# Q's first block from exact codes, an earlier copy of the attention's output, and one block of Q's products ahead of O's first unit

## The chip, the cores and the metric

The kernel runs on one core of a Trainium2 chip. The metric is the time of one execution on the device in microseconds (us), the median of several runs. PE is TensorE (PEld its weight loads), DVE is VectorE, ACT is ScalarE, POOL is GpSimd and SP is SyncE, which here only issues DMAs.

## The reference

One decoder layer on x of shape (2, 512, 1024): attention with 32 query and 8 key/value heads of width 128 and weights given as 4-bit codes with one scale for each block of 128 input rows and each output column, a product with a quantised context, and a layer with binarised weights.

```python
def _dequant(codes, scales):
    w = codes.astype(jnp.float32) - 8.0
    return w * jnp.repeat(scales, GS, axis=0)          # GS = 128

q = hidden_states @ _dequant(q_codes, q_scales)         # k and v likewise
...
q = _rope(q); k = _rope(k)
k = jnp.repeat(k, rf, axis=1); v = jnp.repeat(v, rf, axis=1)
scores = jnp.einsum('bhqd,bhkd->bhqk', q, k) * scale + mask[None, None]
attn = jax.nn.softmax(scores, axis=-1)
out = jnp.einsum('bhqk,bhkd->bhqd', attn, v)
return out.transpose(0, 2, 1, 3).reshape(b, s, NH * HD) @ _dequant(o_codes, o_scales)
...
x = x + attn(layernorm(x))
x = x + matmul(fake_quant(layernorm(x)), fake_quant(ctx))
x = x + einsum('bsi,oi->bso', layernorm(x), binarize(weight))
```

## The kernel before

Most of the time goes into 64 **slots**, one for each pair of head and batch: p = 8g + i, with the key/value head g, the head h = i // 2 of its four, and the batch b = i % 2, so that even slots have b = 0. Slots 8 to 39 (g from 1 to 4, a hardware loop) also quantise a piece of the context; they are called context slots here. Slots 0 to 7 and 40 to 63 (g = 5 to 7) prepare the last layer's weights instead; they are called weight slots. Every engine has its own instruction stream, written out by hand in its own `slot` function, and the streams meet in semaphores. There is no scheduler: the order in the text is the order on the engine.

Values are kept as two float16 halves, upper and lower, and a product of two such numbers is three matmuls (`three_products`: upper x upper, upper x lower, lower x upper). A code itself is exact in one half, so a product with it is two matmuls (O's units do that).

In slot p, PE computes: the scores of p in three parts (`scores` 0, 1, 2, into a pair of PSUM banks that alternate), four of O's units of older heads (`o_unit`, 4 matmuls each; the first of them has index 3 of slot p-1), Q's products for slot p+2 (`q_part`: blocks 0 to 7 of the input, 3 matmuls each, 24 in all, summed in PSUM bank `q_ps`), and at the end the product of the probabilities of slot p-1 with V (`weigh`, 12 matmuls, into `pv_ps`). `scores` 2 of a slot waits for ACT's first exponential of the same slot, whose bank it takes.

Between these, for each slot: DVE takes the maxima of the scores (`maxima`), adds O's units to `x_acc` (`o_add`), scales Q's weights (`piece_scale`) and makes their lower half (`piece_lo`). ACT takes the exponentials (`exps`), makes upper halves of the weights (`q_cut`), of Q (`q_hi`), of the probabilities (`prob_split`, parts 0 and 1) and of the attention's output (`ao_part`), and turns O's codes into float16 (`o_cut`). POOL normalises the probabilities (`norm`, four instructions), makes their lower half (`prob_rest`, parts 0 and 1) and that of Q (`q_lo`). In weight slots DVE also runs `wf_lower` and `wf_difference`, POOL `wf_clip` and `wf_add`. `ao_rest` on DVE makes the lower half of the attention's output from `pv_ps`.

The rotary step on Q of slot p+2 runs after its last product: ACT swaps the halves (`q_swap`, two copies of 64 rows), POOL multiplies by the sine (`sine`), DVE by the cosine in place in `q_ps` (`q_cos`), and in the next slot DVE adds the two into `rot` (`q_sum`), ACT and POOL split `rot` into `q_sb` (`q_hi`, `q_lo`). The first product of Q's next slot waits for `q_sum`, which frees `q_ps`.

## Time and profile before

| | us |
|---|---|
| median of 3 runs | 1098.23 (1096.35 to 1099.12) |
| the profiled execution | 1096.75 |
| span of its trace, first to last instruction | 1095.0 |
| PE busy | 1050.8 (96%) |
| DVE busy | 930.0 (85%) |
| POOL busy | 721.3 (66%) |
| ACT busy | 692.5 (63%) |
| PE's granted clock, mean | 0.998 of full speed |
| 32 context slots | 387.9, 12.12 each |
| 22 weight slots, 40 to 61 | 263.9, 12.00 each |

The end of one slot is seen best in `weigh`, of which there is one for each slot. The first slots begin at about 183 us, slot 63 ends at about 946 us; before them lie the layer norm and the products of K and V, behind them the last two layers. A row of a timeline gives start, duration, engine, line and names; in brackets stands how long the engine was idle before it, and which instruction ended that. On ACT, DVE and POOL the recorded duration of an instruction reaches some 0.03 to 0.1 us into the next one, so a step is read from start to start.

### The profile page before, as it was taken

The page shows a single profiled execution, that of the slowest core. Times are in us where ns is not written, and L with a number is a line of the kernel's source. Part 1 is how long each engine was busy: PE and PEld are TensorE (multiplying, and loading weights), DVE is VectorE, ACT ScalarE, POOL GpSimd, SP SyncE. Part 2 cuts the span into 40 slices and gives each one's busy share as a digit, 9 for nine tenths or more (in the row PEclk, how much of TensorE's full clock was granted, in tenths as well). Part 3 has the DMA queues.
Part 4 walks back from the last instruction along what each step waited for, and adds up shares of the span by engine and source line. Part 5 has one row for each costly group of instructions (what it writes and reads, how often), then busy time and mean ns, then how long its engine had stood idle before and what let it go on. Part 6 is the DMA issues. An engine that isn't in the chain of part 4 may idle for free.

```text
span 1095.0 us, 18877 instructions
## 1 busy us (share of the span) xinstructions
PE 1050.8 (96%) x5416; PEld 507.9 (46%) x5416; DVE 930.0 (85%) x1738; ACT 692.5 (63%) x1499; POOL 721.3 (66%) x789
## 2 busy tenths in 40 slices
PE   5999998999999999999999999999999999889998
PEld 3433433455444444444444444445444544444443
DVE  7967998799888888888888889999999998888873
ACT  5536766766777777777777776666666666463320
POOL 4659887877777677767776777788778877332200
PEclk9999999999999999999999999999999999999999
DMA  9664321777776676667666766777867665532443
GB/s 340 205 162 147 97 73 40 166 146 158 154 161 135 156 155 159 137 154 161 151 139 155 161 148 132 153 158 156 149 157 167 143 134 118 108 117 57 99 98 84
DMA packets 309652, 155.74 MB, mean 142 GB/s; under 512 B 257712, under 2 KB 270256, under 8 KB 309584
## 3 DMA queue, kind: packets, MB, share of 16 engines
q1 hardware_dynamic: 301808, 141.56, 56.6%
q10 hardware_dynamic: 7776, 13.37, 4.4%
q8 instruction: 31, 0.51, 0.2%
q14 instruction: 37, 0.30, 0.1%
HBM read 89.07 MB, written 4.19 MB: 85 GB/s over the span
## 4 chain that ended last, share of the span: by engine, by line
PE 73%; DVE 9%; ACT 6%; POOL 5%; issue 3%; DMA 1%; ACTq 1%; SPq 1%; DVEq 0%; POOLq 0%
PE side_ps L721 9%; PE side_ps L893 9%; PE side_ps L723 9%; PE side_ps L722 9%; PE proj_ps L913 8%; PE out_ps L913 8%; PE proj_ps L1064 4%; PE score_ps L876 3%; PE score_ps L877 2%; PE score_ps L878 2%; PE proj_ps L1069 2%; PE score_ps L1035 2%; DVE stats L1755 1%; ACT prob L1240 1%; DVE x_acc L2022 1%
## 5 line engine op out<-in xcount | busy, mean ns | idle before, releaser
L1587 POOL TENSOR_TENSOR w_b<-prob,w_b 128x896 f16<-128x896 f32 (+2 forms) x192 | 189.0, 999 | 29.8 <-ACT w_b L1267 29.5
L721 PE MATMUL side_ps<-hT,w_a 128*128 128x512 f16 x504 | 191.1, 379 | 1.5 <-DVE rot L1942 1.5
L723 PE MATMUL side_ps<-hT,w_a 128*128 128x512 f16 x504 | 191.0, 379 | 0.0
L722 PE MATMUL side_ps<-hT,w_a 128*128 128x512 f16 x504 | 191.0, 379 | 0.0
L1580 POOL TENSOR_SCALAR prob<-prob,row_inv 128x512 f32<-128x512 f32 (+3 forms) x256 | 170.9, 682 | 23.3 <-DVE row_inv L2095 17.9
L2022 DVE SCALAR_TENSOR_TENSOR x_acc<-proj_ps,o_now,x_acc 128x1024 f32<-128x1024 f32 x120 | 153.5, 1279 | 38.3 <-PE proj_ps L913 38.3
L1240 ACT ACTIVATE prob<-score_ps,neg_max 128x512 f32<-128x512 f32 (+3 forms) x256 | 133.0, 522 | 47.3 <-DVE neg_max L1998 39.0
L1594 POOL TENSOR_TENSOR q_sb<-rot,q_sb 128x512 f16<-128x512 f32 x62 | 72.3, 1167 | 137.3 <-ACT q_sb L1230 137.3
L2022 DVE SCALAR_TENSOR_TENSOR x_acc<-out_ps,o_now,x_acc 128x1024 f32<-128x1024 f32 x120 | 152.6, 1272 | 0.0
L913 PE MATMUL out_ps<-work,w_b 128*128 128x512 f16 x496 | 127.3, 379 | 2.0 <-DVE x_acc L2022 2.0
L913 PE MATMUL proj_ps<-work,w_b 128*128 128x512 f16 x496 | 127.3, 379 | 1.9 <-DVE x_acc L2022 1.1
L1998 DVE CUSTOM_DVE_ANT_0 score_ps<-score_ps,mask_b 128x512 f32<-128x512 f32 (+3 forms) x256 | 121.9, 496 | 2.0 <-PE score_ps L878 2.0
L1267 ACT ACTIVATE w_b<-prob 128x896 f16<-128x896 f32 (+2 forms) x192 | 99.5, 552 | 32.7 <-POOL prob L1580 30.5
L893 PE MATMUL side_ps<-work,v_sb 128*128 128x512 f16 (+3 forms) x768 | 114.8, 299 | 0.0
L1575 POOL TENSOR_TENSOR swapped<-swapped,sin_t 128x512 f32<-128x512 f32 x77 | 99.9, 1297 | 0.1
L893 PEld LDWEIGHTS side_ps<-work,v_sb 128*128 128x128 f16 (+1 forms) x768 | 69.7, 98 | 44.8 <-DMA work<-w_b 0.4
L1276 ACT ACTIVATE work<-side_ps 128x512 f16<-128x512 f32 x64 | 38.2, 597 | 72.5 <-PE side_ps L893 72.4
L876 PE MATMUL score_ps<-k_sb,q_sb 128*128 (+4 forms) x256 | 76.9, 300 | 4.7 <-ACT prob L1240 2.2
L721 PEld LDWEIGHTS side_ps<-hT,w_a 128*128 128x128 f16 x504 | 49.2, 98 | 65.7 <-issue 10.8
L723 PEld LDWEIGHTS side_ps<-hT,w_a 128*128 128x128 f16 x504 | 49.3, 98 | 59.5
L913 PEld LDWEIGHTS out_ps<-work,w_b 128*128 128x128 f16 x496 | 48.3, 98 | 61.1 <-DVE x_acc L2022 3.5
L877 PE MATMUL score_ps<-k_sb,q_sb 128*128 (+4 forms) x256 | 76.6, 299 | 0.0
(259 smaller groups left out, 2108.6 us busy)
## 6 DMA issues: line engine op xcount, KB each, us to landing
stage_c<-in_codes_dram SPq DMA_DIRECT2D x72, 256.0 KB, 2.9
stage_o<-in_codes_dram SPq DMA_DIRECT2D x64, 256.0 KB, 3.9
stage_s<-in_scales_dram SPq DMA_DIRECT2D x64, 256.0 KB, 3.8
ctx_raw<-in_ctx_dram ACTq DMA_DIRECT2D x32, 256.0 KB, 3.3
work<-w_b SPq DMA_TRANSPOSE x261, 3.0
x_acc<-in_x_dram SPq DMA_DIRECT2D x8, 512.0 KB, 8.3
k_sb<-in_codes_dram SPq DMA_DIRECT2D x16, 256.0 KB, 7.0
v_sb<-in_scales_dram SPq DMA_DIRECT2D x16, 256.0 KB, 7.2
```

Source lines behind the costliest of these rows:

```text
L721: pe.matmul(o, stat(0), mov(0), start=first, stop=False)
L722: pe.matmul(o, stat(0), mov(1), start=False, stop=False)
L723: return pe.matmul(o, stat(1), mov(0), start=False, stop=last)
L876: pe.matmul(o, q[0], k[0], start=True, stop=False)
L893: mm = pe.matmul(pv_ps[:, kb * P:S], v_sb[:, bass.ds(g, 1), l, b * TB + kb, :].rearrange("p a d -> p (a d)"), probT[:, m, at:kb + (TB - 1) ...
L913: mm = pe.matmul(o[:, b, :], o_codes[:, h % RING, cb * P:(cb + 1) * P], ao[:, h % 2, l, b * S:(b + 1) * S], start=l == 0, stop=l == 1)
L1240: ins = act.activation(prob[:, SCORE_AT[qb]:SCORE_AT[qb] + w], score_ps[:, score_bank(i, u), off:off + w], ACT.Exp, bias=neg_max[:, c:c + ...
L1575: pool.tensor_tensor(y, y, sin_t[:, :], ALU.mult).then_inc(done, 1)
L1580: return pool.tensor_scalar(prob[:, at:at + w], prob[:, at:at + w], row_inv[:, col:col + 1], P_UP, ALU.mult, ALU.mult)
L1587: ins = pool.tensor_tensor(prob16[:, 1, to:to + w], prob[:, at:at + w], prob16[:, 0, to:to + w], ALU.subtract)
L1998: ins = dve.tensor_tensor_reduce(s, s, mask_b[:, S - w:S], -1.0, MAX_FROM, ALU.add, ALU.min, neg_max[:, c:c + 1])
L2022: ins = dve.scalar_tensor_tensor(y, u, s, y, ALU.mult, ALU.add)
```

## The change

1. **Exact codes.** From Q's slot 4 on (`by_parts`), block 0 of Q's weights is kept as codes minus 8 in the upper half alone. PE multiplies it in two matmuls instead of three (`q_exact`), into `pv_ps` instead of `q_ps`. ACT scales the result with the column scales while it copies it to SBUF (`q_base`; the tile is the second half of `stage_o`), DVE adds the sum of blocks 1 to 7 to it (`q_join`). ACT's `q_swap` and the cosine then read SBUF. The cosine moves from DVE (`q_cos`) to POOL (`q_turn`, in the next slot), `q_sum` adds two tiles of SBUF. In every second slot `piece_scale` and `piece_lo` cover 384 columns instead of 512, and ACT's piece is two instructions (128 and 384 columns).
2. **ACT's order.** `ao_part` stands ahead of `q_swap`, which now waits for `q_join`; `o_cut` moves from behind `prob_split` 1 to ahead of `prob_split` 0; `q_hi` moves behind the last exponential.
3. **PE's order.** Block 1 of Q stands ahead of O's unit 0, block 0 and block 2 behind it, all ahead of `scores` 2; before, one block stood there.
4. **DVE's and POOL's order.** `ao_rest` of slot p-2 stands behind the first maxima of slot p instead of at the end of slot p-1; `q_sum` stands behind the last maxima; `piece_lo` behind `o_add` 1. On POOL `sine` and `q_turn` stand at the slot's start, `q_lo` behind the first two norms.
5. O's codes have one buffer instead of two, loaded once `o_cut` has read it. One DMA more (Q's scales, 128 x 256 words) and three small DVE instructions fill a table ahead of the slots.

```diff
+EXACT = P
+EARLY = 2
+Q_LEAD = 3
@@ SyncE @@
+            sp.dma_start(q_scale_rows, q_scales).then_inc(scale_rows_landed, 16)
...
+            def next_o(g, i):
...
+                sp.wait_ge(o_codes_done, p + 1)
+                load_o(o_index(*after), (i + 1) % 2)
@@ TensorE @@
+            def q_exact(g, i):
+
+                h = i // B
+                p = g * SLOTS + i
+                pe.wait_ge(piece_done, g * SLOTS + (2 * h + 2))
+                pe.wait_ge(ao_ready, p - 3)
+                for l in range(2):
+                    mm = pe.matmul(pv_ps, w_a[:, 0, h % RING * KB * P:(h % RING * KB + 1) * P],
+                                   hT[:, l, 0, i % B * S:(i % B + 1) * S], start=l == 0, stop=l == 1)
+                mm.then_inc(q_exact_done, 1)
...
-                        pe.wait_ge(q_summed, p)
+                        pe.wait_ge(q_joined, p - FIRST_PIECES)
...
                     pe.wait_ge(ao_ready, p)
+                if not (known(p) and (p == 0 or p >= N_SLOTS - FIRST_PIECES + 1)):
+                    pe.wait_ge(q_based, p)
...
+                if has_ahead and parts:
+                    q_part(*ahead, range(1, EARLY))
                 if has_o:
                     o_unit(p, i, 0)
-                if has_ahead:
+                if has_ahead and parts:
+                    q_exact(*ahead)
+                elif has_ahead:
                     q_part(*ahead, range(0, 1))
+                if has_ahead and parts:
+                    q_part(*ahead, range(EARLY, 3))
                 scores(p, i, g, 2)
-                if has_ahead:
+                if has_ahead and not parts:
                     q_part(*ahead, range(1, 3))
@@ ScalarE @@
+                if by_parts(p):
+                    act.wait_ge(q_joined, p - FIRST_PIECES + 1)
+                swap(q_swap_of(p), q_sum_in if by_parts(p) else q_bank(p), q_swapped)
+
+            def q_base(g, i):
+
+                p = g * SLOTS + i
+                act.wait_ge(q_exact_done, p - FIRST_PIECES + 1)
+                if not (known(p) and p == FIRST_PIECES):
+                    act.wait_ge(q_cosed, p)
...
+                act.activation(q_sum_in, pv_ps, ACT.Copy, scale=o_now[:, (i // B + 1) % 2, CB:CB + 1])\
+                    .then_inc(q_based, 1)
@@ GpSimd @@
+            def q_turn(p):
+
+                pool.wait_ge(q_joined, p - FIRST_PIECES + 1)
+                pool.wait_ge(q_ready, p)
+                pool.tensor_tensor(rot[:, :], q_sum_in, cos_t[:, :], ALU.mult).then_inc(q_cosed, 1)
@@ VectorE @@
-                dve.tensor_tensor(q_rot(p), q_bank(p), q_swap_of(p), ALU.add).then_inc(q_summed, 1)
+                dve.tensor_tensor(q_rot(p), rot[:, :] if by_parts(p) else q_bank(p), q_swap_of(p), ALU.add)\
+                    .then_inc(q_summed, 1)
+
+            def q_join(p):
+
+                dve.wait_ge(q_done, p + 1)
+                dve.wait_ge(q_based, p - FIRST_PIECES + 1)
+                dve.tensor_tensor(q_sum_in, q_bank(p), q_sum_in, ALU.add).then_inc(q_joined, 1)
```

The order on ACT in a weight slot, from `exps` 2 to the first exponential of the next slot (`stage_s` to `w_a` is the piece, `stage_o` to `w_b` is `o_cut`, `prob` to `w_b` is `prob_split`, `side_ps` to `work` is `ao_part`, into `swapped` goes `q_swap`). Before:

```order
L1240 ACTIVATE prob,row_sum<-score_ps,neg_max 128x256
L1143 ACTIVATE w_a<-stage_s 128x512
L1302 ACTIVATE w_b<-w_b 128x256
L1267 ACTIVATE w_b<-prob 128x896
L1148 ACTIVATE swapped<-side_ps 64x512
L1149 ACTIVATE swapped<-side_ps 64x512
L1276 ACTIVATE work<-side_ps 128x512
L1267 ACTIVATE w_b<-prob 128x128
L1267 ACTIVATE w_b<-prob 128x256
L1253 ACTIVATE w_b<-stage_o 128x512
L1240 ACTIVATE prob,row_sum<-score_ps,neg_max 128x512
```

and with the change:

```order
L1294 ACTIVATE prob,row_sum<-score_ps,neg_max 128x256
L1284 ACTIVATE q_sb<-rot 128x512
L1182 ACTIVATE w_a<-stage_s 128x512
L1356 ACTIVATE w_b<-w_b 128x256
L1307 ACTIVATE w_b<-stage_o 128x512
L1321 ACTIVATE w_b<-prob 128x896
L1330 ACTIVATE work<-side_ps 128x512
L1187 ACTIVATE swapped<-stage_o 64x512
L1188 ACTIVATE swapped<-stage_o 64x512
L1321 ACTIVATE w_b<-prob 128x128
L1321 ACTIVATE w_b<-prob 128x256
L1294 ACTIVATE prob,row_sum<-score_ps,neg_max 128x512
```

The swap now lies behind `ao_part` and ahead of `prob_split` 1, and O's codes are cut before both.

The order on POOL in a weight slot, from `prob_rest` 0 (128x896) of one slot to the norms of the next (`wf_add` and `wf_clip` are `w_b` from `w_b`, 128x256). Before:

```order
L1587 TENSOR_TENSOR w_b<-prob,w_b 128x896
L1575 TENSOR_TENSOR swapped<-swapped,sin_t 128x512
L1587 TENSOR_TENSOR w_b<-prob,w_b 128x128
L1587 TENSOR_TENSOR w_b<-prob,w_b 128x256
L1673 TENSOR_TENSOR w_b<-w_b 128x256
L1648 TENSOR_SCALAR w_b<-w_b 128x256
L1594 TENSOR_TENSOR q_sb<-rot,q_sb 128x512
L1580 TENSOR_SCALAR prob<-prob,row_inv 128x512
L1580 TENSOR_SCALAR prob<-prob,row_inv 128x384
```

and with the change:

```order
L1644 TENSOR_TENSOR w_b<-prob,w_b 128x896
L1644 TENSOR_TENSOR w_b<-prob,w_b 128x128
L1644 TENSOR_TENSOR w_b<-prob,w_b 128x256
L1736 TENSOR_TENSOR w_b<-w_b 128x256
L1632 TENSOR_TENSOR swapped<-swapped,sin_t 128x512
L1652 TENSOR_TENSOR rot<-stage_o,cos_t 128x512
L1711 TENSOR_SCALAR w_b<-w_b 128x256
L1637 TENSOR_SCALAR prob<-prob,row_inv 128x512
L1637 TENSOR_SCALAR prob<-prob,row_inv 128x384
L1657 TENSOR_TENSOR q_sb<-rot,q_sb 128x512
```

The sine has moved behind `prob_rest` 1, the cosine is new behind it, and `q_lo` has moved behind two norms.

The order on DVE in a weight slot, from the last maxima to the last `o_add`. Before:

```order
L1998 ISA score_ps,neg_max<-score_ps,mask_b 128x256
L1998 ISA neg_max 128x1
L2095 RECIPROCAL row_inv<-row_sum 128x3
L1782 SCALAR_TENSOR_TENSOR stage_s<-stage_c,stage_s 128x512
L2099 RECIPROCAL row_inv<-row_sum 128x1
L1966 SCALAR_TENSOR_TENSOR w_b<-w_b 128x256
L1788 SCALAR_TENSOR_TENSOR w_a<-stage_s,w_a 128x512
L2022 SCALAR_TENSOR_TENSOR x_acc<-out_ps,o_now,x_acc 128x1024
L1960 SCALAR_TENSOR_TENSOR w_b<-w_b,wf_mean 128x256
L2022 SCALAR_TENSOR_TENSOR x_acc<-proj_ps,o_now,x_acc 128x1024
```

and with the change:

```order
L2081 ISA score_ps,neg_max<-score_ps,mask_b 128x256
L2081 ISA neg_max 128x1
L2010 TENSOR_TENSOR rot<-rot,swapped 128x512
L2187 RECIPROCAL row_inv<-row_sum 128x3
L1850 SCALAR_TENSOR_TENSOR stage_s<-stage_c,stage_s 128x512
L2191 RECIPROCAL row_inv<-row_sum 128x1
L2049 SCALAR_TENSOR_TENSOR w_b<-w_b 128x256
L2105 SCALAR_TENSOR_TENSOR x_acc<-out_ps,o_now,x_acc 128x1024
L1856 SCALAR_TENSOR_TENSOR w_a<-stage_s,w_a 128x512
L2043 SCALAR_TENSOR_TENSOR w_b<-w_b,wf_mean 128x256
L2017 TENSOR_TENSOR stage_o<-side_ps,stage_o 128x512
L2105 SCALAR_TENSOR_TENSOR x_acc<-proj_ps,o_now,x_acc 128x1024
```

`q_sum` stands ahead of the reciprocals that POOL's norms wait for, and `piece_lo` (L1856) behind an `o_add`.

## Rows read from the trace of the kernel before

**Rows 1.** The page: busy time, share of the span and instructions of each engine.

```profile
PE 1050.8 (96%) x5416; PEld 507.9 (46%) x5416; DVE 930.0 (85%) x1738; ACT 692.5 (63%) x1499; POOL 721.3 (66%) x789
```

**Rows 2.** The chain that ended last, in order of time: start us, us, what.

```profile
220.36 1.63 PE side_ps L893 x12
232.26 1.63 PE side_ps L893 x12
...
268.23 1.63 PE side_ps L893 x12
...
656.12 1.64 PE side_ps L893 x12
...
920.02 1.64 PE side_ps L893 x12
...
1010.88 3.45 PE score_ps L1035 x16
```

**Rows 3.** Timeline of PE in a context slot: start us, us, engine, line, operation.

```profile
318.00 0.38 PE L876 MATMUL score_ps<-k_sb,q_sb 128*128 x1
...
321.94 0.28 PE L876 MATMUL score_ps<-k_sb,q_sb 128*128 x1
```

**Rows 4.** Timeline of ACT in the same context slot.

```profile
318.28 0.60 ACT L1276 ACTIVATE work<-side_ps 128x512 f16<-128x512 f32 x1 [1.18 <-PE side_ps L893]
318.77 0.61 ACT L1267 ACTIVATE w_b<-prob 128x128 f16<-128x128 f32 x2
319.28 0.62 ACT L1253 ACTIVATE w_b<-stage_o 128x512 f16<-128x512 int32 x1
...
321.11 0.69 ACT L1240 ACTIVATE prob<-score_ps,neg_max 128x512 f32<-128x512 f32 x1 [0.69 <-ACT k_sb L1363]
```

**Rows 5.** Timeline of POOL in a weight slot.

```profile
777.73 1.26 POOL L1575 TENSOR_TENSOR swapped<-swapped,sin_t 128x512 f32<-128x512 f32 x1
779.26 1.06 POOL L1587 TENSOR_TENSOR w_b<-prob,w_b 128x128 f16<-128x128 f32 x2 [0.27 <-ACT w_b L1267]
780.28 0.74 POOL L1673 TENSOR_TENSOR w_b<-w_b 128x256 f32<-128x256 f32 x1
780.98 0.41 POOL L1648 TENSOR_SCALAR w_b<-w_b 128x256 f32<-128x256 f32 x1
782.92 1.16 POOL L1594 TENSOR_TENSOR q_sb<-rot,q_sb 128x512 f16<-128x512 f32 x1 [1.54 <-ACT q_sb L1230]
784.32 3.02 POOL L1580 TENSOR_SCALAR prob<-prob,row_inv 128x512 f32<-128x512 f32 x4 [0.23 <-DVE row_inv L2095]
787.60 1.90 POOL L1587 TENSOR_TENSOR w_b<-prob,w_b 128x896 f16<-128x896 f32 x1 [0.26 <-ACT w_b L1267]
```

**Rows 6.** Timeline of DVE in the same weight slot.

```profile
778.71 0.69 DVE L2038 SCALAR_TENSOR_TENSOR work<-side_ps,work 128x512 f16<-128x512 f32 x1 [0.37 <-ACT work L1276]
779.32 0.69 DVE L1998 CUSTOM_DVE_ANT_0 score_ps<-score_ps,mask_b 128x512 f32<-128x512 f32 x1
...
783.98 0.17 DVE L2095 RECIPROCAL row_inv<-row_sum 128x3 f32<-128x3 f32 x1
```

**Rows 7.** Groups on DVE, weight slots 656.12 to 920.02: busy us, mean ns, idle before.

```profile
L1966 DVE SCALAR_TENSOR_TENSOR w_b<-w_b 128x256 f16<-128x256 f32 x21 | 14.7, 702 | 0.0
L1788 DVE SCALAR_TENSOR_TENSOR w_a<-stage_s,w_a 128x512 f16<-128x512 f32 x20 | 13.8, 692 | 0.5 <-ACT w_a L1143 0.5
L1782 DVE SCALAR_TENSOR_TENSOR stage_s<-stage_c,stage_s 128x512 f32<-128x512 int32 x20 | 13.1, 656 | 0.0
```

**Rows 8.** Single lines of DVE with both inputs in SBUF: duration ns min/median/max.

```profile
L1813 DVE TENSOR_TENSOR rot<-rot,swapped x15: 671/693/1752, 78.3 to 174.3; 128x512 f32<-128x512 f32 x15
L1960 DVE SCALAR_TENSOR_TENSOR w_b<-w_b,wf_mean x31: 466/469/1705, 184.1 to 938.8; 128x256 f32<-128x256 f32 x31
```

**Rows 9.** Timeline of DVE: the first maxima of slots 62 and 63.

```profile
922.92 0.69 DVE L1998 CUSTOM_DVE_ANT_0 score_ps<-score_ps,mask_b 128x512 f32<-128x512 f32 x1
...
932.26 0.68 DVE L1998 CUSTOM_DVE_ANT_0 score_ps<-score_ps,mask_b 128x512 f32<-128x512 f32 x1
```

More of the change, by code:

```diff
@@ L462, in build @@
         cc_ready = sem("cc_ready")
-        xs_landed = [sem(f"xs_landed{t}") for t in range(TT)]
         y_turned = sem("y_turned")
@@ L1338, in slot @@
                 exps(p, i, 2)
+                if has_next and by_parts(p + 1):
+                    q_hi(p + 1)
                 if has_piece:
@@ L1344, in slot @@
                     wf_sign(wf_early(p))
+                o_cut(p, i)
                 prob_split(p, 0)
@@ L1348, in slot @@
                     act.activation(ctx_raw[:, :], ctx_raw[:, :], ACT.Copy, bias=ROUND).then_inc(ctx_rounded, 1)
+                if has_prev and not (known(p) and p == N_SLOTS - 1):
+                    ao_part(p - 1, (i - 1) % SLOTS)
                 if has_ahead:
@@ L1356, in slot @@
                     return
-                if has_prev:
-                    ao_part(p - 1, (i - 1) % SLOTS)
                 prob_split(p, 1)
-                o_cut(p, i)
                 if with_ctx:
@@ L1691, in body @@
                     norm(2).then_inc(norm_done, 1)
+                    if not (known(p) and p >= N_SLOTS - 1) and by_parts(p + 1):
+                        q_lo(p + 1)
                     if with_ctx:
@@ L2075, in slot @@
                     j = o_scales(g, i)
-                if i or known(p):
+                first = not (i or known(p))
+                if not first:
+                    maxima(p, i, 0)
+                if first:
+                    dve.wait_ge(q_ready, p + 1)
+                if has_prev and p_ge2:
+                    ao_rest(p - 2, (i - 2) % SLOTS)
+                if first:
                     maxima(p, i, 0)
@@ L2091, in slot @@
                 maxima(p, i, 2)
+                if has_next and by_parts(p + 1):
+                    q_sum(p + 1)
                 if known(p) and p < 3:
@@ L2101, in slot @@
                     wf_lower(wf_late(p))
-                if has_piece:
-                    piece_lo(n, i % 2, q_region(i), Q_UP)
                 if has_o:
                     o_add(p, i, 1)
+                if has_piece:
+                    piece_lo(n, i % 2, q_region(i), Q_UP, (EXACT, 0)[i % B])
                 if known(p) and wf_early(p) is not None:
                     wf_difference(wf_early(p))
+                if has_ahead and by_parts(p + Q_AHEAD):
+                    q_join(p + Q_AHEAD)
                 if has_o:
```

107 lines of the change are left out of this document (65 added, 42 removed).

## Prediction

> **What bounds the kernel now.** Read the page's busy times first: PE is busy for 96% of the span, DVE for 85% [rows 1]. Then read the chain in order of time for the spacing of `weigh`, one in each slot. The closest neighbours are 11.90 us apart (220.36 to 232.26), and this is PE without a pause: 40 matmuls of 512 columns at 0.216 (16 of them take 3.45) are 8.64, `weigh` is 1.63, and the scores have as many columns as `weigh` [rows 2]. So 11.90 is PE's floor. Context slots, 268.23 to 656.12, take 387.89 for 32, or 12.12 each; the 22 weight slots up to 920.02 take 263.90, or 12.00 each [rows 2]. The loop is bound by PE, with 0.22 and 0.10 lost in a slot. Where a context slot loses it the timeline shows: with T for the start of `scores` 0, `scores` 2 begins at T + 3.94 (318.00, 321.94) [rows 3], while the work ahead of it (scores 1.30, two O units 1.73, one block 0.65, all at 0.216 for a full matmul [rows 2]) ends at T + 3.68. It starts 0.83 after the first exponential (T + 3.11) does [rows 4]: PE waits for ACT there.
>
> **The change, part by part.**
>
> *PE.* Two matmuls instead of three in 60 slots (2 to 61) are 60 x 0.216 = 12.9 us where PE is the bound. The floor goes to 11.90 - 0.22 = 11.68. With one more matmul pair and two more blocks, less the old one, `scores` 2 now comes naturally at T + 1.30 + 1.73 + 1.29 + 0.43 = T + 4.75.
>
> *ACT, context slots.* Behind `weigh`, ACT ran `ao_part` (T + 0.28), `prob_split` 1, `o_cut` (0.52 from start to start), the context's last copy, a DMA issue and the exponential [rows 4]. Now the swap's two copies come in, and `o_cut` leaves. For a copy I take `ao_part`'s 0.60 without a gap, so 1.21 for both. The exponential begins at T + 3.11 + 1.21 - 0.52 = T + 3.80, and `scores` 2 may start 0.83 later, at T + 4.63. PE comes at 4.75: no wait, with 0.12 to spare. Other waits of a context slot: POOL runs `prob_rest` 1 at T + 2.7 (0.7 behind the split, which starts at T + 1.99), the sine from T + 3.7, the new cosine until T + 6.3. DVE can be there at T + 5.5 and waits, adds, and its slot still closes by T + 12.3, that is 0.6 into the next slot, before scores are there for it (0.85: 0.65 of matmuls and the tail of the last). `q_lo` ends near T + 10.1, ahead of PE's next slot at 11.68. The context slots go to the floor: 387.89 - 32 x 11.68 = **14.1 us less**. `q_base` (a copy from PSUM, 0.60) and the split piece hide in ACT's idle time, 37% of the span [rows 1]; without it they would push the exponential by up to 0.8.
>
> *Weight slots.* The same walk, from rows of one such slot. POOL: `prob_rest` 1 at T + 2.7, its step 1.02 and `wf_add` 0.70 to T + 4.4, then sine and cosine, 1.27 each less an overlap of 0.03: done at T + 6.9. The cosine has no row in the slots; the sine, the same operation on the same size, is the nearest, and I take its time [rows 5]; a tenth more moves everything below by 0.1. DVE: from the first maxima to the reciprocal is 4.66 (779.32 to 783.98), with a `q_sum` in it (0.61 by its step) that an `ao_rest` of the same step (778.71 to 779.32) replaces [rows 6]. DVE could be at `q_sum` by T + 0.85 + 4.66 = T + 5.5, so it waits until T + 6.95. Behind it stand, by steps (durations less 0.08): `q_sum` 0.61 (0.693), two reciprocals 0.17, `piece_scale` 0.58 and `piece_lo` 0.54 (from 0.656 and 0.692, three quarters in every second slot), `wf_lower` 0.62 (0.702), `wf_difference` 0.40 (median 0.469), `q_join` 0.61 (as long as `ao_rest`, which also reads PSUM), half of an `o_now` copy 0.16, and two `o_add` of 1.19: 6.07 [rows 6 to 8]. The last two, and all O units below, have no row of their own: an `o_add` is what is left of the 4.66 behind three maxima and a `q_sum`, halved. So maxima begin at T + 13.0, 1.35 into the next slot. `ao_rest` is done at 1.35 + 0.60 + 0.69 = 2.64, ahead of O's first unit at 2.81, which waits for it in odd slots. By this the weight slots are at the floor, by 0.17.
>
> What could use up those 0.17 is the meeting of DVE and POOL. An addition with both inputs in SBUF took 0.693 us as median, but up to 1.752, and `wf_difference` 0.469, but up to 1.705 [rows 8]; the first is as fast as `ao_rest` with an input in PSUM (0.69) [rows 6] when nothing is in its way. In the change `q_sum` becomes such an addition and starts as the cosine ends, when POOL goes straight on to `wf_clip` (0.41) [rows 5]: up to 0.33 more. `piece_lo`, now behind an `o_add`, begins at about T + 10.5. POOL gets its reciprocal at T + 8.2, takes two norms of 0.75 (3.02 for four) and is in `q_lo` (1.16) from T + 9.7 to 10.9 [rows 5]: up to 0.4 more. With both, `ao_rest` is done at 2.64 + 0.73 = 3.37 and the unit waits 0.6 in every odd slot, so a pair takes 2 x 11.68 + 0.6 = 24.0, and a slot 12.0. The rows bound this cost between 0 and 1.24 (1.705 less 0.469) for each of these instructions. I take the overlaps as they fall in the walk, because rows 8 show that such instructions do wait: 22 slots at 12.0 are 264.0, **nothing gained or lost**. The four slots 4 to 7 (47.87) are of the same kind: 0. Slots 2 and 3 give 2 x 0.216 = **0.4 less**.
>
> The Trainium skill bears on this (SBUF — State Buffer, section "Who interferes with whom"): a DVE instruction with two SBUF inputs and a GpSimd instruction that reads SBUF take the same read interface, and whichever is second waits until the first is finished. The maxima of rows 8 agree with it, the medians show how rarely it happened. By the rule the weight slots come out at 12.0, without it at 11.68.
>
> *The end.* Slot 62 has no Q products, so it is short: its first maxima and those of slot 63 are 9.34 apart [rows 9]. With the change DVE must wait for the cosine in it until T + 6.95, and then still has `q_sum` 0.94, reciprocals 0.17, `wf_lower` 0.4, `o_add` 1.19, `wf_difference` 0.40 behind POOL's `q_lo` (about 0.9 of waiting), `o_add` 1.19 and the copy: maxima at T + 12.4 against 1.2 in slot 62, so 11.2 apart: 1.9 more. Slot 63 also has two `ao_rest` in place of one, 0.6. PE waits for `q_lo` meanwhile (T + 10.7). **2.5 us more.** Nothing reduces this, since the end of the slots is bound by DVE.
>
> *Costed at nothing.* DVE's three small instructions and the added DMA lie ahead of the slots beside PE's products of K; their bounds are 0 and 3 x 0.4 us. The single buffer of O's codes: loading starts at T + 10.3 and is needed one slot later. The change in SP's order leaves each load several us.
>
> **Sum:** -14.1 + 0 - 0.4 + 2.5 = -12.0 us. Against the profiled execution's 1096.75 this is 1084.8; that execution lies 1.5 under the median 1098.23, so the median becomes **1086.2**.
>
> **The rivals.**
>
> *B, POOL and DVE don't meet.* Then the weight slots reach 11.68: 263.9 - 257.0 = 6.9 less, slots 4 to 7 1.2 less, together -20.1: 1078.1. For it speaks the median of 0.693; against it that the cosine's end releases `q_sum` and `wf_clip` together. 0.15.
>
> *C, a second wait in the context slots.* The spare 0.12 ahead of `scores` 2 is thin. If the swap, the split piece or the context's clip (which moved behind `q_lo`) costs 0.2 more than walked, each of 32 slots gives 0.2 back: -12.0 + 6.4, 1092.6. For it: before, PE waited 0.26 in this very place. 0.19.
>
> *D, slower.* POOL's longest instruction, `prob_rest` 0, reads SBUF and takes 1.90 [rows 5]. In the walk `wf_difference` starts at T + 11.5 and `prob_rest` 0 at T + 12.5. If DVE lags 1.0 more than walked, `wf_difference` or `piece_lo` falls behind it and waits about half, 0.95, in each of 26 weight slots; from then on each lag brings the next. -12.0 + 24.7 = +12.7: 1110.9. For it: an excess of 1.24 does occur [rows 8]. Against it: PE's wait holds both engines back equally, so the phase between DVE and POOL scarcely drifts. 0.12. The Trainium skill's rule in the section named above would make the wait the whole rest of POOL's instruction, up to 1.90.
>
> **How the numbers follow.** The forecast has 0.54. What a measurement of this kernel can tell from no change is about 0.3%, 3.3 us, so "faster" means under 1094.9. Faster: 0.54 + 0.15 + 0.13 of C = 0.82. Same: 0.06 of C. Slower: 0.12. The range takes in B and C with the bounds of the meeting costs and leaves out D and the edges of C: 1077.5 to 1096.
>
> **What would show it.** Context slots: `weigh` 11.68 apart over all 32, no idle on PE ahead of `scores` 2. Weight slots: even slots 11.7, odd ones about 12.3, PE idle ahead of O's first unit with DVE's `ao_rest` as its releaser, DVE's `q_sum` released by POOL's cosine and about 0.3 longer than in context slots. Slot 62 near 11 us instead of 8.5. If context slots show 11.9, C holds; if weight slots show 11.7 throughout, B; if `wf_difference` has a mean over 1 us, D. The forecast is wrong altogether if `q_lo` becomes what `scores` 0 waits for in ordinary slots, since then POOL's chain sets the period.

## The result, and the profile after

The changed kernel takes 1103.95 us (1101.56 to 1108.18) against 1097.78 (1096.35 to 1099.12) for the kernel before: a ratio of 1.006, with a 95% interval of 1.004 to 1.0081. Forecast were 1086.2, with 1077.5 to 1096.0 as the range. So the forecast was wrong in sign: 12 us less was expected, and it became 6 us more. The profiled execution took 1102.88. One execution of the second experiment took 1559.15 us at a mean granted clock of 0.656, where its other three had 0.995 to 0.997; it is left out, and the time given there, 1087.91, is the median of those three, where a later expectation has 1088.6 with it.

First the page, as in [rows 1], with the shares of the chain and a line from its table of queues (packets, MB, share), which was `q14 instruction: 37, 0.30, 0.1%` before:

```profile
PE 1040.0 (94%) x5346; PEld 503.7 (46%) x5356; DVE 957.8 (87%) x1741; ACT 726.5 (66%) x1589; POOL 784.1 (71%) x849
...
q14 instruction: 68, 0.56, 0.2%
...
POOL 50%; issue 17%; DVE 13%; PE 13%; ACT 3%; DMA 1%; SPq 1%; POOLq 0%; DVEq 0%; ACTq 0%
```

PE works 10.8 us less, as intended. DVE is busy 27.8 us longer with three instructions more. That is the first hint: some instruction of DVE has become long.

Where in the program the time goes is read from the starts of `weigh`, as in [rows 2]. PE's timeline of the changed kernel, at the same three borders:

```profile
268.62 1.79 PE L923 MATMUL side_ps<-work,v_sb 128*128 128x512 f16 x12
...
658.06 1.79 PE L923 MATMUL side_ps<-work,v_sb 128*128 128x512 f16 x12
...
922.98 1.79 PE L923 MATMUL side_ps<-work,v_sb 128*128 128x512 f16 x12
```

| from `weigh` to `weigh` | before | forecast | after |
|---|---|---|---|
| slots 2, 3 | 24.00 | 23.6 | 24.28 |
| slots 4 to 7 | 47.87 | 47.9 | 48.34 |
| context slots (32) | 387.89 | 373.8 | 389.44 |
| weight slots (22) | 263.89 | 264.0 | 264.92 |
| slots 62, 63 | 19.96 | 22.5 | 23.16 |

The context slots are the miss: 15.7 of the 18 us. Even ones (b = 0) mostly came out at 11.79, odd ones between 12.29 and 12.42, where all were to be at 11.68. The loop over the context groups returns to its start three times; the first slots behind a return (16, 24, 32) took 12.45, 12.75 and 12.71, and the odd ones that follow them (17, 25, 33) 12.12, 13.20 and 12.38.

What PE waited for in the context slots (line waited for: us in total, times, longest) names the two places:

```profile
PE proj_ps L943 <- DVE work L2121: 8.8, 16, 1.3
PE score_ps L904 <- ACT prob L1294: 2.4, 3, 0.9
```

The first is O's first unit, waiting for `ao_rest` (L2121) in each of the 16 odd slots. The second is `scores` 2 in the three slots behind a return, which come further down. For the first, the timelines of DVE, POOL and PE in one of the odd slots show why:

```profile
305.33 1.27 DVE L2105 SCALAR_TENSOR_TENSOR x_acc<-proj_ps,o_now,x_acc 128x1024 f32<-128x1024 f32 x1
306.52 1.55 DVE L2091 COPY o_now<-work 128x9 f32 x1
307.99 0.68 DVE L2081 CUSTOM_DVE_ANT_0 score_ps<-score_ps,mask_b 128x512 f32<-128x512 f32 x1
...
308.59 0.68 DVE L2121 SCALAR_TENSOR_TENSOR work<-side_ps,work 128x512 f16<-128x512 f32 x1
```

```profile
306.16 1.88 POOL L1644 TENSOR_TENSOR w_b<-prob,w_b 128x896 f16<-128x896 f32 x1
```

```profile
309.52 1.03 PE L943 MATMUL proj_ps<-work,w_b 128*128 128x512 f16 x4 [0.46 <-DVE work L2121]
```

The copy that brings nine scales from the table to `o_now` took 1.55 us. POOL's `prob_rest` 0 began 0.36 before it and ended at 308.04, the copy at 308.07: it stood behind POOL's instruction to its very end. The views of the single line, over the 16 odd context slots and over 11 weight slots (ns, min/median/max):

```profile
L2091 DVE COPY o_now<-work x16: 1547/1552/1555, 282.4 to 647.8; 128x9 f32 x16
```

```profile
L2091 DVE COPY o_now<-work x11: 512/516/860, 672.4 to 913.6; 128x9 f32<-128x9 f32 x11
```

The 16 long ones began 0.36 or 0.37 behind `prob_rest` 0. Of the 11 in weight slots, 10 began 1.40 behind it (743.73 and 745.13 in one) and took 0.52. All 26 ended 0.02 to 0.04 behind POOL's instruction: the copy took what was left of it.

In the kernel before the same view over the context slots read 391/393/395 ns, for 8 words. The copy stood behind `ao_rest` there, and the one at 283.12 began 0.06 behind POOL's `prob_rest` 1, whose two pieces of 128 and 256 columns take 1.06 together.

### The profile page after: what moved, and what is told of

Same layout as the page of the kernel before. It is cut to its first block, busy times and chain, and to the rows that moved or that the text cites. A ratio compares the mean times of both kernels' runs of the same rounds, so it can differ in the third digit from the quotient of the medians.

```text
span 1101.1 us, 19064 instructions
## 1 busy us (share of the span) xinstructions
PE 1040.0 (94%) x5346; PEld 503.7 (46%) x5356; DVE 957.8 (87%) x1741; ACT 726.5 (66%) x1589; POOL 784.1 (71%) x849
## 4 chain that ended last, share of the span: by engine, by line
POOL 50%; issue 17%; DVE 13%; PE 13%; ACT 3%; DMA 1%; SPq 1%; POOLq 0%; DVEq 0%; ACTq 0%
POOL w_b L1644 14%; POOL prob L1637 12%; POOL swapped L1632 7%; POOL rot L1652 5%; POOL q_sb L1657 4%; PE proj_ps L1101 4%; DVE rot L2010 3%; POOL ctx_raw L1763 2%; PE proj_ps L1106 2%; PE score_ps L1072 2%; POOL w_b L1736 2%; DVE x_acc L2105 1%; DVE stats L1823 1%; DVE v_sb L1862 1%; POOL rot L1680 1%
## 5 line engine op out<-in xcount | busy, mean ns | idle before, releaser
L1637 POOL TENSOR_SCALAR prob<-prob,row_inv 128x512 f32<-128x512 f32 (+3 forms) x256 | 166.1, 660 | 69.2 <-DVE row_inv L2187 63.4
L737 PE MATMUL side_ps<-hT,w_a 128*128 128x512 f16 x444 | 168.4, 379 | 0.0
L738 PE MATMUL side_ps<-hT,w_a 128*128 128x512 f16 x444 | 168.4, 379 | 0.0
L739 PE MATMUL side_ps<-hT,w_a 128*128 128x512 f16 x444 | 168.3, 379 | 0.0
L943 PE MATMUL proj_ps<-work,w_b 128*128 128x512 f16 x496 | 127.4, 379 | 20.9 <-issue 11.2
L2081 DVE CUSTOM_DVE_ANT_0 score_ps<-score_ps,mask_b 128x512 f32<-128x512 f32 (+3 forms) x256 | 122.1, 497 | 13.0 <-PE score_ps L906 11.2
L943 PEld LDWEIGHTS proj_ps<-work,w_b 128*128 128x128 f16 x496 | 45.9, 97 | 86.7 <-issue 34.4
L904 PE MATMUL score_ps<-k_sb,q_sb 128*128 (+4 forms) x256 | 76.8, 300 | 3.6 <-ACT prob L1294 3.5
L905 PE MATMUL score_ps<-k_sb,q_sb 128*128 (+4 forms) x256 | 76.6, 299 | 0.0
L1652 POOL TENSOR_TENSOR rot<-stage_o,cos_t 128x512 f32<-128x512 f32 x60 | 76.3, 1271 | 0.0
L906 PE MATMUL score_ps<-k_sb,q_sb 128*128 (+4 forms) x256 | 73.3, 299 | 0.0
```

What stands on the lines that cost most here:

```text
L737: pe.matmul(o, stat(0), mov(0), start=first, stop=False)
L738: pe.matmul(o, stat(0), mov(1), start=False, stop=False)
L739: return pe.matmul(o, stat(1), mov(0), start=False, stop=last)
L943: mm = pe.matmul(o[:, b, :], o_codes[:, h % RING, cb * P:(cb + 1) * P], ao[:, h % 2, l, b * S:(b + 1) * S], start=l == 0, stop=l == 1)
L1637: return pool.tensor_scalar(prob[:, at:at + w], prob[:, at:at + w], row_inv[:, col:col + 1], P_UP, ALU.mult, ALU.mult)
L1652: pool.tensor_tensor(rot[:, :], q_sum_in, cos_t[:, :], ALU.mult).then_inc(q_cosed, 1)
```

## The experiments

Every ratio is to the kernel before, run again beside the experiment (medians 1096.7 to 1098.3). The experiments go by their numbers; there is no seventh.

**Is it the copy?** Theory L: the copy is held behind `prob_rest` 0 and makes `ao_rest` late. Rival R: POOL's chain (norms, `q_lo`, sine, cosine), which fills half of the new page's chain of work, sets the period. The first experiment moves the copy behind the first maxima:

```
-                if has_o and i % B:
-                    j = o_scales(g, i)
                 first = not (i or known(p))
 ...
+                if has_o and i % B:
+                    j = o_scales(g, i)
                 if first:
```

(and the same in slot 63, which has lines of its own).

> The changed kernel, with one thing moved: DVE's copy of O's scales (o_now, 9 words, in odd slots) stands behind the first maxima instead of ahead of them, where POOL's prob_rest 0 is over. Theory L (the copy waits behind prob_rest 0 and makes DVE late for ao_rest): the copy's median falls from 1.55 to below 0.5, odd slots fall from 12.3-12.5 to 11.8-11.9, PE's wait ahead of O's first unit goes, and the time falls from 1104 by 30 slots x 0.6 and 1.3 at the end, to 1083 to 1088. Theory R (POOL's longer chain, with the cosine, sets the period and the copy only fills time that DVE would wait anyway): the pairs stay at 24.1 and the time within 2 us of 1104.

Measured: 1089.45 us, 1.5 above the upper end of what was expected, ratio 0.9937 (0.9921 to 0.9954); context slots 380.62, weight slots 261.46. PE's wait for `ao_rest` in the context slots shrank from 8.8 us to 0.8, though POOL's instructions are the same. So L holds and R falls. The copy still met POOL at times (159/422/1097 ns).

The second leaves the copy in its place and writes it as a sum over an axis of length 1:

```
-                dve.tensor_copy(o_now[:, of[1] % 2, :],
-                                o_table[...].rearrange("p h c -> p (h c)"))
+                dve.tensor_reduce(o_now[:, of[1] % 2, :],
+                                  o_table[...].rearrange("p h c -> p c h"), AX_X, ALU.add)
```

> The changed kernel with the copy of O's scales in its old place, written as a reduction over an axis of length 1, the same 9 words in and out. Theory L in its narrow form (a plain copy takes an interface that POOL's instruction holds; a reduction does not): 0.2 us or less instead of 1.55, and the same 1083 to 1088 as with the copy moved. If the copy is late for any other reason that lies in its place (its address from a register, the fetch of its instruction), the reduction takes 1.5 too and the time stays at 1104.

Measured: 1087.91, ratio 0.9926 (0.9906 to 0.9946). The single line:

```profile
L2091 DVE TENSOR_REDUCE o_now<-work x32: 145/147/151, 209.1 to 926.2; 128x9 f32<-128x9 f32 x16, 128x9 f32 x16
```

Same place, same address, same nine words, while POOL runs `prob_rest` 0 as before: 0.147 instead of up to 1.7 us, each time. It is the form of the instruction, and one line of code is worth about 15 us (16.0 between the medians, 14.7 by the two ratios). The Trainium skill states this (SBUF — State Buffer, section "Who interferes with whom"): a copy can take the ports that DVE shares with GpSimd, so that whoever comes second is blocked for the whole instruction of the other, while a `tensor_reduce` never contends on trn2. The trace agrees with both halves: 1552 ns against 147.

**What does the old kernel get without exact codes?** The third experiment is the kernel before with two of Q's blocks, not one, ahead of `scores` 2, which removes the wait of [rows 3, 4] and nothing else:

```
-                    q_part(*ahead, range(0, 1))
+                    q_part(*ahead, range(0, 2))
                 scores(p, i, g, 2)
                 if has_ahead:
-                    q_part(*ahead, range(1, 3))
+                    q_part(*ahead, range(2, 3))
```

> The kernel before with one part of the change alone: two of Q's blocks instead of one ahead of scores 2, all behind O's first unit, and nothing else. scores 2 then comes naturally 0.65 us later, behind the 0.27 that PE waited there. My theory: context slots fall from 12.12 to 11.90 and weight slots from 12.00 to 11.93, together 32 x 0.22 + 22 x 0.07 = 8.6 less, 1089.5. Rival: the later scores 2 make the last exponential, q_cut and piece_lo late by the same 0.4, and DVE, which has 1 us to spare, passes it on: within 2 us of 1098.

Measured: 1088.4, ratio 0.9931 (0.9911 to 0.995), 1.1 under what was expected. All but a few slots stand at 11.89. So the wait for ACT was read rightly, and moving one block brings 8 us, where 12 were forecast for the whole change.

The twelfth experiment adds the reduction to it, in the same form as above.

> The third experiment (the kernel before with two of Q's blocks ahead of scores 2, 1088.4 us) with the o_now copy written as a reduction. In the kernel before the copy stands behind ao_rest and took 0.15 to 0.74 us; with two blocks ahead of scores 2 it took 0.16 in weight slots and PE is at its floor of 11.89 in nearly all slots. If the form matters only where the copy meets POOL's prob_rest, nothing is won here: 1088.4 within 0.7. If a reduction is also better in itself, up to 0.2 us in each of 31 slots on DVE, which PE would not show either. More than 2 us less than 1088.4 would mean that I misread what ends a slot there.

Measured: 1087.89, ratio 0.9906 (0.9892 to 0.992): no difference clear of noise. The traces show a small one. In the third experiment the odd slots 9, 17, 25 and 33 took 12.06 to 12.09, with a copy of 0.39 to 0.41, where it took 0.24 or 0.25 in the other context slots; with the reduction they took 11.89 or 11.90, 0.7 us less together. In slot 3, where the copy took its longest, 0.742, the reduction brought 0.5. In nearly all other slots the copy made nothing late.

**The odd weight slots.** They were at 12.15 without the copy's delay. In the changed kernel POOL waits for the first reciprocal ahead of its norms 62 times, 63.4 us in all. The fourth experiment is the first with that reciprocal ahead of `q_sum` instead of behind it:

```
-                if has_next and by_parts(p + 1):
-                    q_sum(p + 1)
                 ...
                 dve.reciprocal(row_inv[:, 0:3], row_sum[:, 0:3]).then_inc(inv_ready[0], 1)
+                if has_next and by_parts(p + 1):
+                    q_sum(p + 1)
```

> The first experiment (copy behind the first maxima) and, besides, DVE's reciprocal of the row sums ahead of q_sum instead of behind it, so that POOL's norms don't wait for q_sum. Theory L: POOL is not the bound once the copy is free, so the gain over the first experiment is small, 0 to 3 us (a little in slot 62, where DVE waits 1.3 for the cosine). Theory R: POOL's wait ahead of its norms, 1.04 in each slot, falls by 0.6, and 60 x 0.6 = 36 us would come off wherever POOL sets the period. A loss is possible if the norms now take the interface first and q_sum waits 0.6 behind them.

Measured: 1087.31, ratio 0.9911 (0.9894 to 0.9928); odd weight slots 12.00. That is 2.1 us less than the first, so the 36 us of theory R are ruled out. The fifth has this place of the reciprocal, the copy back in its old place, and the copy written as a reduction.

> The changed kernel with the o_now copy written as a reduction (as in the second experiment) and the reciprocal of row_sum 0:3 ahead of q_sum (as in the fourth). If the two are independent: the reduction alone gave 1088.6, the reciprocal's place took weight slots from 12.15 to 12.00 at odd b (11 slots x 0.15 = 1.6 us), so 1087.0, with odd weight slots at 12.00, context slots as in the second experiment (11.79 and 11.70), 3 loop boundaries still at 12.7. If DVE's queue, not the lateness of POOL's norm, sets the odd weight slots once the copy is short, nothing changes: 1088.6 and 12.14.

Measured: 1084.74, ratio 0.9891 (0.9876 to 0.9906); odd weight slots 12.00 again, 2.3 below what was expected.

**The slots behind a return of the loop.** In the fifth they stood at 12.78, 12.75 and 12.68. DVE's and ACT's timelines there:

```profile
364.70 0.69 DVE L2121 SCALAR_TENSOR_TENSOR work<-side_ps,work 128x512 f16<-128x512 f32 x1 [1.71 <-issue]
```

```profile
365.11 0.61 ACT L1420 ACTIVATE v_sb<-ctx_raw 128x512 f32 x1
366.88 0.35 ACTq L1377 DMA_DIRECT2D ctx_raw<-in_ctx_dram  x1
367.41 0.69 ACT L1294 ACTIVATE prob<-score_ps,neg_max 128x512 f32<-128x512 f32 x1 [1.69 <-issue]
```

Both engines stand still at the first instructions of the body, for nothing that the profile shows; in other slots ACT's DMA issue follows 0.16 behind the copy's end, here 1.16. And the queue of instructions moved 31 packets more than before. The sixth experiment takes two waits out of `q_sum` that others imply, which makes the body of DVE's loop 263 instructions long instead of 271 in the built program (262 before):

```
-                dve.wait_ge(q_sined, p + 1)
+                if not by_parts(p):
+                    dve.wait_ge(q_sined, p + 1)
                 dve.wait_ge(q_cosed, p + 1)
                 ...
-                elif not (known(p) and p < Q_AHEAD):
+                elif not by_parts(p) and not (known(p) and p < Q_AHEAD):
                     dve.wait_ge(q_ready, p)
```

> The fifth experiment with two waits that are implied by others taken out of q_sum (POOL's q_turn, whose semaphore q_sum still waits for, comes behind the sine and behind q_ready), in blocks whose Q comes by parts. It shortens the body of DVE's loop over the context groups from 271 instructions to 263 in the built program; in the kernel before it has 262. Theory X (the body of DVE's loop has become too long and is fetched anew at each return: packets of the queue of instructions 37 before, 68 after): packets fall back to about 37, the wait of 2.2 us ahead of the first ao_rest of a round goes, the three slots behind a return fall from 12.7 to 11.9, so 2.5 us less than the fifth, about 1084.5. Theory Y (the length has nothing to do with it: the return itself takes this long, and before the change it was hidden because ao_rest stood ahead of it): packets stay at 68, 12.7 stays, and the time is that of the fifth experiment within 0.5 us.

Measured: 1084.89, ratio 0.9884 (0.9869 to 0.9899); packets 53; the slots behind a return 12.71, 12.67 and 12.66. Half of X came true: 15 packets and DVE's wait are gone, as the same row shows, now released by ACT's copy:

```profile
364.26 0.69 DVE L2122 SCALAR_TENSOR_TENSOR work<-side_ps,work 128x512 f16<-128x512 f32 x1 [0.30 <-ACT work L1330]
```

But the median is the same as the fifth's: the first maxima of that slot ended at 365.56, and the exponential that needs them began at 368.29, behind ACT's own stop. `scores` 2 waits for that exponential. (The context slots of this trace took 378.63, those of the fifth 380.07, because slots 25 and 33 took 11.78 instead of 12.48 and 12.33. In the second experiment, where DVE stopped as in the fifth, they took 11.78 too, so this is not shown to be DVE's stop.)

The ninth tests X from the other side: the third experiment, where nothing stops, with 16 instructions more in DVE's loop body:

```
+                dve.wait_ge(const_ready, 2)
+                dve.wait_ge(scal_ready, 1)
+                dve.wait_ge(mean_ready, 1)
                 if has_o:
                     o_add(p, i, 1)
```

(and the same ahead of `o_add` 2).

> The third experiment (the kernel before with two of Q's blocks ahead of scores 2, 1088.4 us, slots behind a return of the loop 12.06, 37 packets of the queue of instructions) with 16 instructions more in the body of DVE's loop that do nothing but test semaphores that rose long ago: 278 instead of 262. Theory X (a longer body is fetched anew at each return): packets rise to about 60 to 70, the slots behind a return go from 12.06 to 12.5 or more, and the time rises by 1 to 3 us, beside some tenths for the tests themselves. Theory Y (the length has nothing to do with it): 37 packets, 12.06, and 1088.4 within 0.7 us.

Measured: 1088.42, ratio 0.9919 (0.9906 to 0.9933); 38 packets, and slots 4 to 59 all within 0.02 of the third's. (The 12.06 of the expectation belongs to the second slot behind a return, as in the third; the first, which is the long one in the changed kernel, stood at 11.89 in both.) Length alone isn't it. The place differs too: the extra tests also stand in slots 0 to 7, ahead of the loop, and had moved the body. The thirteenth experiment has the same body of 278 instructions with fewer tests ahead of it, and none behind it:

```
-                dve.wait_ge(const_ready, 2)
-                dve.wait_ge(scal_ready, 1)
-                dve.wait_ge(mean_ready, 1)
+                if not known(p) or p in (3, 4):
+                    dve.wait_ge(const_ready, 2)
+                    dve.wait_ge(scal_ready, 1)
+                    dve.wait_ge(mean_ready, 1)
```

> The ninth experiment (the kernel before with two of Q's blocks ahead of scores 2 and 16 tests of long risen semaphores in the body of DVE's loop, 278 instructions, no more packets than before) with fewer such tests ahead of the loop, so that the same 278 instructions stand elsewhere: as instructions 561 to 838 of DVE's program in the built program, where they were 585 to 862. Bodies that showed no added packets so far: 553 to 814, 557 to 819 and 585 to 862; with added packets and the wait of 2.2 us on DVE: 562 to 832. Theory Z (what decides is which boundaries between blocks of the program the body covers, not its length alone; with blocks of 128 and three of them kept, a boundary at 820 to 832 divides the cases): this body covers a fourth block, packets rise from 38 to about 53, DVE idles 1 to 2 us at 3 returns, and the slots behind them go from 12.06 to 12.5 or more; 1089 to 1090.5. Rival (the place is nothing, and something else in the changed kernel's body makes the packets): 38 packets, 12.06, and 1088.4 within 0.7.

Measured: 1100.33, ratio 1.003 (1.0019 to 1.004). Its queue of instructions, and DVE's and PE's waits (PE's in the context slots):

```profile
q14 instruction: 52, 0.43, 0.1%
```

```profile
DVE rot L1942 <- issue: 9.4, 3, 3.1
```

```profile
PE side_ps L721 <- DVE rot L1942: 6.9, 3, 2.3
```

Twelve us more than the ninth, from where the same instructions stand. The packets came out as Z says; the price was about six times the highest that was expected. Slots 16, 24 and 32 took 14.56, 14.54 and 15.99 instead of 11.89, 9.4 us together, as much as DVE stood still; every other slot from 2 to 61 is within 0.04 of the ninth's. DVE's cases compare as follows:

| body in DVE's program | instructions | packets of the queue | DVE's wait at a return |
|---|---|---|---|
| before, third: 553 to 814 | 262 | 37 | none |
| sixth: 557 to 819 | 263 | 53 (68 less 15) | none |
| ninth: 585 to 862 | 278 | 38 | none |
| after, fifth: 562 to 832 | 271 | 68 | 6 us in 3 |
| thirteenth: 561 to 838 | 278 | 52 | 9.4 us in 3 |

The bodies that stop begin at 561 or 562 and end at 832 or later; those that begin earlier and end by 819, or begin at 585, don't stop. That the place makes the stop is shown by the ninth and the thirteenth; what exactly the border is, five cases don't fix. The Trainium skill (Runtime: NRT & Kernel Launch, section "Instruction fetch mechanics") says that an engine other than PE keeps only two blocks of 256 instructions and that a branch to one that isn't there stops it until it is fetched. The table can be read so: with a border between 819 and 832, and so another between 563 and 576, the bodies that stop lie over three such blocks and the others over two. The runs measure neither the size of a block nor how many are kept; the blocks of 128 of the expectation, three of them kept, divide the five cases in the same way. Whether ACT's stop is the same was tried in the tenth, by shortening its body, on top of the eighth:

```
-                act.wait_ge(q_done, p + 1)
+                if not by_parts(p):
+                    act.wait_ge(q_done, p + 1)
 ...
-                elif not (known(p) and p < Q_AHEAD):
+                elif not by_parts(p) and not (known(p) and p < Q_AHEAD):
                     act.wait_ge(q_summed, p)
 ...
-                free = (q_done, p + (RING - i % B))
+                free = None if not known(p) else (q_done, p + (RING - i % B))
```

> The eighth experiment with the waits taken out of ScalarE's program that others imply (q_done and q_summed ahead of the swap, since q_joined implies both; q_done ahead of the cut of a piece, since the swap a slot earlier had waited for more). The body of ScalarE's loop over the context groups goes from 319 instructions to 303 in the built program; the kernel before has 293. Theory: the 16 packets of the queue of instructions that are left over the 37 of the kernel before (53 in the sixth and eighth) are ScalarE's loop body, fetched anew at the 3 returns, and the 1.6 us from its last ctx operation to the next ctx DMA there (0.78 in other slots) are that fetch. Then the packets fall to about 37, that stretch falls to 0.8, the 3 slots behind a return go from 12.03 (mean of 12.16, 12.03, 12.00) to 11.7, and the time falls by about 1 us to 1079.4. Rival: the stretch is the return itself, whatever the length: packets 53, 12.03, and 1080.4 within 0.5.

Measured: 1082.39, ratio 0.9855 (0.9839 to 0.987), against 1080.39 and 0.9846 for the eighth, which follows below; packets 53, and the slots behind a return 12.17, 12.75, 12.40. Nothing was won: a miss. Its body, 442 to 744 of ACT's program instead of 448 to 766 (432 to 724 before), may still lie over a border of its own; no run moves it, so for ACT the cause stays open.

**The second wait.** The even context slots stood at 11.79, with 0.11 of waiting ahead of `scores` 2 by the theory, as in rival C. The eighth puts a third block ahead of it, on top of the sixth:

```
-                    q_part(*ahead, range(EARLY, 3))
+                    q_part(*ahead, range(EARLY, 4))
 ...
-                    q_part(*ahead, range(3, KB))
+                    q_part(*ahead, range(4 if parts else 3, KB))
```

> The sixth experiment with three of Q's blocks instead of two between scores 1 and scores 2 (besides the exact one). If the even context slots stand at 11.79 because exp 1 is 0.11 late ahead of scores 2, they fall to 11.68: 16 x 0.11 = 1.8 us less than the sixth. If what is given comes back because scores 2, and with it exp 2, the second reciprocal and POOL's norm, come 0.65 us later, weight slots of odd b rise by up to 0.3 (11 x 0.3 = 3.3 us) and the time is 1.5 us above the sixth.

Measured: **1080.39** (1079.59 to 1081.57), ratio 0.9846 (0.9833 to 0.986): context slots 375.16, nearly all at 11.68, and the weight slots as they were (259.86); only slots 2 and 3 are 0.65 longer together. So the 0.11 was the wait ahead of `scores` 2. The block also took 0.6 from each slot behind a return, which wasn't expected: 4.5 us less than the sixth, where 1.8 was the theory. This is the best version, 8 us under the third experiment, the kernel before with one block moved. That is what exact codes and the new orders bring together once the copy, the reciprocal and the third block are out of their way; no run separates the codes from the orders.

**The place of `piece_lo`.** The prediction charged 0.4 for its meeting with `q_lo` behind an `o_add`. The eleventh is the tenth with `piece_lo` back ahead of that `o_add`:

```
-                if has_o:
-                    o_add(p, i, 1)
                 if has_piece:
                     piece_lo(n, i % 2, q_region(i), Q_UP, (EXACT, 0)[i % B])
+                if has_o:
+                    o_add(p, i, 1)
```

> The tenth experiment with DVE's piece_lo back ahead of the o_add of O's unit 1, where it stood before the change. What the prediction charged for its new place is the meeting with POOL's q_lo: 1.01 us for 512 columns in the trace of the eighth, against 0.69 where nothing meets it. If the old place is free of POOL, DVE's round of two weight slots is 0.3 to 0.5 us shorter and odd weight slots fall from 12.00 to 11.7 to 11.8: 2 to 3 us less than the tenth. If piece_lo now meets POOL's norm instead (which runs at that moment in the trace of the eighth) or waits for ScalarE's cut with DVE idle behind the second reciprocal, DVE loses as much or more: the same time, or up to 3 us more.

Measured: 1125.28, ratio 1.0261 (1.0239 to 1.0283), with odd weight slots mostly at 14.3 to 16.0: 43 us more than the tenth, fourteen times the worst that was expected. DVE's timeline in one of these slots, then POOL's and PE's:

```profile
772.37 1.26 DVE L1858 SCALAR_TENSOR_TENSOR w_a<-stage_s,w_a 128x384 f16<-128x384 f32 x1 [0.64 <-ACT w_a L1183]
773.55 1.27 DVE L2108 SCALAR_TENSOR_TENSOR x_acc<-out_ps,o_now,x_acc 128x1024 f32<-128x1024 f32 x1
774.75 1.71 DVE L2046 SCALAR_TENSOR_TENSOR w_b<-w_b,wf_mean 128x256 f32<-128x256 f32 x1
```

```profile
774.29 1.88 POOL L1646 TENSOR_TENSOR w_b<-prob,w_b 128x896 f16<-128x896 f32 x1
```

```profile
779.63 1.86 PE L943 MATMUL proj_ps<-work,w_b 128*128 128x512 f16 x4 [1.61 <-DVE work L2124]
```

`piece_lo` waits 0.64 for ACT's cut, which the change has put behind `q_hi`, and meets `q_lo` all the same (1.26). With that lag `wf_difference` falls behind `prob_rest` 0 and takes 1.71 instead of 0.58, and `ao_rest`, which the last row waits for, is late. This is the mechanism of the prediction's rival D: a lag, then the rest of POOL's instruction. Of the 42.5 us that the slots lost against the tenth, 34 lie in weight slots. The other 8.5 lie in the context slots, which have no `wf_difference`; there PE waited 6.6 for `ao_rest`, in all 16 odd slots. The change's order avoids this, and that part of the walk was right.

## Why the prediction was wrong

**The floor: right.** 11.68 is where a slot stands once nothing waits; it was reached in even weight slots at once and in nearly all context slots in the eighth experiment.

**The context slots (-14.1): the step that failed.** The walk said that DVE's slot "still closes by T + 12.3, that is 0.6 into the next slot, before scores are there for it". It left out what DVE issues between that close and the maxima in odd slots, the copy to `o_now`, and left out what POOL runs then, `prob_rest` 0. The collisions were searched among instructions with both inputs in SBUF only; a copy has one. In the weight slots the walk charged "half of an `o_now` copy 0.16", so 0.32 for one, and in the context slots it doesn't name it. Its own durations in the kernel before were 151/392/740 ns, from what it takes alone to nearly five times that, and none of the prediction's rows has them. Its price was 1552 ns in 16 slots. Of the 15.7 us missed here the reduction gave back 10.6 (389.44 to 378.83).

**The rest of the 15.7.** Three slots behind a return lost about 1.0 each: 3.2 of the 5.1 that were left in the second experiment. The prediction had no step for where the code stands. The even slots' 0.11 is rival C at half its price and in every second slot: the spare of 0.12 ahead of `scores` 2 was not there (1.4 in all).

**Rival D: right mechanism, wrong instruction.** It said that DVE might fall behind `prob_rest` 0 and wait; it named `wf_difference` and `piece_lo`, put the lag that this needs at 1.0, and gave it a chance of 0.12. The copy stood there with no lag at all.

**The weight slots (0): nearly right, partly by the reasons given.** Even ones 11.68 as walked, odd ones 12.50 for 12.3. The groups that answer to [rows 7, 8], from 656 to 928 in the changed kernel (ns, min/median/max):

```profile
L2010 DVE TENSOR_TENSOR rot<-rot,swapped x22: 822/824/827, 666.2 to 919.6; 128x512 f32<-128x512 f32 x22
```

```profile
L1856 DVE SCALAR_TENSOR_TENSOR w_a<-stage_s,w_a x21: 873/1004/1480, 656.8 to 898.9; 128x512 f16<-128x512 f32 x11, 128x384 f16<-128x384 f32 x10
```

`q_sum` takes 0.13 more than alone, for its meeting with `wf_clip` (0.33 was charged). `piece_lo` takes a mean of 1.03 for 512 columns against 0.69 before, 0.34 for its meeting with `q_lo` (0.4). The copy took 0.52; as a reduction it brought these slots to 12.14 and all 22 to 261.3. So the 264.9 that hit the forecast of 264.0 is in part luck: without the copy's excess it would have been 2.7 under it, since the meetings were charged too high.

**The end (+2.5): 3.2.** The copy again, with 1.46 in front of slot 63's first maxima, where [rows 9] had them 9.34 apart, 11.2 were forecast, and it became 12.42 (925.57 to 937.99). DVE's timeline:

```profile
925.57 0.70 DVE L2081 CUSTOM_DVE_ANT_0 score_ps<-score_ps,mask_b 128x512 f32<-128x512 f32 x1 [0.23 <-PE score_ps L906]
...
936.62 1.46 DVE L2091 COPY o_now<-work 128x9 f32<-128x9 f32 x1
937.99 0.68 DVE L2081 CUSTOM_DVE_ANT_0 score_ps<-score_ps,mask_b 128x512 f32<-128x512 f32 x1
```

With the reduction the two slots took 21.85, 1.9 more than before.

**The size of the range.** Its upper end was built from rival C and the meetings of named instructions, and left out rival D. A bound for every instruction of DVE that starts beside POOL's longest would have been 16 x 1.9 for the odd context slots, 30 us, and would have held the result.

## What to carry to other kernels

List every DVE instruction that begins while POOL works, the shortest above all, and ask which ports its form may take: nine words can wait for a whole instruction of the other engine. A small copy between SBUF tiles that must be quick beside POOL is better written as a reduction over an axis of length 1; where it makes nothing late, as in the twelfth experiment, that wins next to nothing. When a loop's body changes, look at the packets of the instruction queue and for waits on nothing ahead of the body's first instructions; where the body stands in its engine's program can matter more than what was changed in it.

## What was not expected of the hardware

- A copy of 9 words in each of 128 partitions took 147 ns as a reduction, and as a copy 1552 ns in 16 slots of 16 behind an instruction of POOL that had begun 0.36 or 0.37 us earlier; the two ended within 0.04 us of each other each time.
- The same 278 instructions of DVE's loop cost nothing at a return as 585 to 862 of its program and 3.1 us at each as 561 to 838, with 14 packets of instructions more.
- Taking DVE's stop away brought nothing (1084.74 and 1084.89) as long as ACT stopped too, with 16 packets left over those of the kernel before. Why ACT did, and whether moving its body would end it, stays open.
